# Scatter-add of scaled routed rows in a mixture-of-experts layer

## The chip, the cores and the metric

The kernel runs on one core of a Trainium2 chip. The metric is device time in microseconds (us) of one execution; before the change the median of three runs is 440.13 us (439.99 to 445.27).

## What is computed

A small vision tower: patches of 64 images are projected to 3136 tokens of 128 channels (B = 64 images, L = 49 tokens each), normalised, mixed along the tokens by a state-space convolution, and passed through a mixture of experts with 2 shared and 8 routed experts, of which each token takes the best two. The change is in this last part:

```python
hs = jax.nn.gelu(jnp.einsum('td,nfd->ntf', t, sw1) + sb1[:, None, :], approximate=False)
shared = jnp.einsum('ntf,ndf->td', hs, sw2) + sb2.sum(axis=0)
logits = t @ gate_w.T + gate_b
probs = jax.nn.softmax(logits, axis=-1)
top_v, top_i = jax.lax.top_k(probs, K)
cw = jnp.zeros_like(probs).at[jnp.arange(T)[:, None], top_i].add(top_v)
hr = jax.nn.gelu(jnp.einsum('td,efd->etf', t, rw1) + rb1[:, None, :], approximate=False)
oe = jnp.einsum('etf,edf->etd', hr, rw2) + rb2[:, None, :]
routed = jnp.einsum('etd,te->td', oe, cw)
return (shared + routed).reshape(b, s, d)
```

The layer's output is added to its input h. T is 3136, K is 2, F is 512.

## The kernel before

**Engines and order.** The program is written by hand: each engine has one list of instructions, and semaphores tie the lists together. Images come in and are projected in four tiles of 16 images (up to about 150 us), then comes the convolution, then the second normalisation (about 190 us) whose rows y are stored to the DRAM tensor yd, one row a token (store_y), and transposed for TensorE.

**Sorting the tokens.** VectorE picks each token's two experts (choose), counts ranks, and gives each of the 6272 (token, choice) pairs a slot in a list sorted by expert (sort_places). one_hots and TensorE's invert turn this into two tables with a column for each tile of 128 slots: take (which row of yd a slot reads) and give (which row of rd it writes); slot_tokens makes them. shares makes cwk, the two softmax shares of each token, for which ScalarE computes the Exp in step S_EXP of its list.

**Routed blocks.** The sorted list is cut into NB = 32 blocks of one expert each: 24 blocks of 256 slots (two tiles) and then 8 blocks of 128 slots (one tile); a table of 32 entries tells each block's expert. ORDER mixes these with the 16 pieces of shared work (8 groups of 392 tokens by 2 experts): 6 pieces first, then one after every three blocks. For a block i:

- SP loads the expert's weights into wb (load_weights, line 505, three buffers), once og of block i - 3 is complete.
- GpSimd gathers the rows of yd into xg, one indirect DMA a tile (gather, line 633, four buffers), and it issues the gather of block i + 4 ahead of the scatter of block i.
- TensorE transposes xg (line 1563), VectorE copies that to x32 (keep_x, line 1193), TensorE multiplies by the first weights (line 1505), ScalarE does the gelu (line 784), and TensorE multiplies by the second weights into PSUM bank 7 (line 1528). It may begin this when VectorE has read the last block's result from the bank.
- VectorE adds the expert's bias and writes og (rows_out, line 1200, two buffers); it waits for the scatter of block i - 2, which read the same buffer, to have landed.
- GpSimd scatters og's rows to rd, one indirect DMA a tile (scatter, line 640). rd has two rows for a token, one for each choice, and a row of its own for each empty slot. These scatters wait for nothing but og.

**The end.** When the last two blocks' scatters have landed, SP loads rk, both rows of each token, in 8 groups (load_routed, line 514, four buffers). ScalarE scales the first rows by their share (scale_routed, line 798), VectorE adds the scaled second rows to h (combine, line 1207) and then ScalarE's part (line 1212) into osb (two buffers), and SP stores osb (line 519) and loads a further group.

## Time and profile before

| | us |
|---|---|
| median of three runs | 440.13 |
| lowest, highest | 439.99, 445.27 |
| profiled execution | 444.05 |
| its span | 442.1 |
| busy: TensorE, ScalarE, VectorE, GpSimd | 364.2, 205.5, 183.0, 174.1 |

The profile is of one execution, which took 444.05 us; the hardware's records of it span 442.1 us. All instants below are counted from the span's start. Busy times leave out the issue of DMAs, except that GpSimd's indirect DMAs are counted while the engine makes them. In an instruction's row, the brackets give the time for which its engine had been idle before it, and what ended that. PE is TensorE, DVE is VectorE, ACT is ScalarE, POOL is GpSimd, and SPq is SP, which only issues DMAs.

### The profile page before, as it was taken

How to read it: one execution, taken by the hardware profiler on the slowest of the kernel's cores; microseconds unless marked ns; L12 is line 12 of the kernel's file. 1: busy time of each engine (PE TensorE's matmuls, PEld its weight loads, DVE VectorE, ACT ScalarE, POOL GpSimd, SP SyncE). 2: the span in 40 equal slices, each digit the busy share in tenths (PEclk: the TensorE clock that was granted, in tenths of full speed). 3: DMA queues.
4: the chain of work that ended last, by engine and by line, in shares of the span. 5: the costliest groups of instructions: out<-in, count | busy, mean ns of one | idle time of the engine just before them, and what ended most of it. 6: DMA issues, size and time to landing. Idle time of an engine off the chain costs nothing.

```text
span 442.1 us, 7120 instructions
## 1 busy us (share of the span) xinstructions
PE 364.2 (82%) x2490; PEld 299.8 (68%) x2490; DVE 183.0 (41%) x579; ACT 205.5 (46%) x424; POOL 174.1 (39%) x226
## 2 busy tenths in 40 slices
PE   0596998998967895839899999999999999989400
PEld 0465856666655784739777878988988988988300
DVE  0473485737769202392787221121121121121166
ACT  2660647837351631445563244554454445455153
POOL 7015134255221230062000357767767767654100
PEclk9995799998995697955798899999999999999855
DMA  8962046930010341022003015425435444455185
GB/s 209 265 191 74 16 131 165 312 128 0 1 71 40 122 150 60 1 74 73 0 33 130 19 42 210 159 101 212 156 128 183 161 146 166 172 173 187 29 278 149
DMA packets 22168, 54.38 MB, mean 123 GB/s; under 512 B 4551, under 2 KB 10109, under 8 KB 22137
## 3 DMA queue, kind: packets, MB, share of 16 engines
q1 hardware_dynamic: 17625, 46.25, 31.8%
q0 software_dynamic: 3968, 7.41, 6.0%
q10 hardware_dynamic: 544, 0.33, 0.4%
q8 instruction: 17, 0.28, 0.3%
q14 instruction: 14, 0.11, 0.1%
HBM read 28.10 MB, written 6.93 MB: 79 GB/s over the span
## 4 chain that ended last, share of the span: by engine, by line
PE 52%; issue 15%; DVE 12%; DMA 8%; POOL 4%; POOLq 3%; DVEq 3%; ACT 3%; SPq 1%; ACTq 0%
PE bank L1528 11%; PE bank L1505 11%; PE bank L1515 8%; DMA Xc<-in_x 3%; PE bank L1267 3%; PE bank L1300 3%; DVE dT L848 2%; PE bank L1480 2%; PE bank L1485 2%; PE bank L1486 2%; PE bank L1487 2%; DMA out<-osb 2%; DMA Tt<-kpad 1%; PE bank L1355 1%; PE bank L1563 1%
## 5 line engine op out<-in xcount | busy, mean ns | idle before, releaser
L633 POOL DMA_INDIRECT xg<-yd,take x56 | 54.5, 974 | 64.1 <-DVE give L1186 47.3
L784 ACT ACTIVATE gf<-bank,wb 128x256 f32<-128x256 f32 (+1 forms) x128 | 51.3, 447 | 52.6 <-PE bank L1505 52.6
L640 POOL DMA_INDIRECT rd<-og,give x56 | 55.2, 986 | 41.4 <-DVE og L1200 28.9
L1528 PE MATMUL bank<-wb,gf 128*128 128x128 f32 x448 | 55.4, 275 | 1.0 <-DVE og L1200 1.0
L1505 PE MATMUL bank<-x,wb 128*128 128x256 f32 (+1 forms) x256 | 54.0, 354 | 2.1 <-issue 1.2
L1528 PEld LDWEIGHTS bank<-wb,gf 128*128 128x128 f32 x448 | 53.2, 192 | 1.5 <-DVE og L1200 1.5
L784 ACT ACTIVATE gf<-bank,vcol 128x392 f32<-128x392 f32 x64 | 35.2, 588 | 36.5 <-PE bank L1487 36.5
L1505 PEld LDWEIGHTS bank<-x,wb 128*128 128x128 f32 x256 | 43.3, 191 | 9.3 <-issue 1.4
L1515 PE MATMUL bank<-gf,ws 128*128 128x392 f32 x128 | 44.8, 492 | 0.0
L1193 DVE COPY x<-bank 128x256 f32<-128x256 f32 (+1 forms) x32 | 12.5, 391 | 65.4 <-PE bank L1563 65.3
L1300 PE MATMUL bank<-patchT,Wp 128*128 128x392 f32 x96 | 38.4, 527 | 0.0
L1200 DVE TENSOR_TENSOR og<-bank,wb 128x256 f32<-128x256 f32 (+1 forms) x32 | 12.5, 390 | 54.6 <-PE bank L1528 50.4
L1515 PEld LDWEIGHTS bank<-gf,ws 128*128 128x128 f32 x128 | 23.3, 190 | 13.4
L1267 PE MATMUL bank<-ident,Xr 112*128 112x112 f32 x168 | 24.0, 288 | 5.6 <-ACT patchT L665 3.7
L1267 PEld LDWEIGHTS bank<-ident,Xr 112*128 112x128 f32 x168 | 19.7, 156 | 11.2 <-issue 6.1
L1485 PE MATMUL bank<-yh,ws 128*128 128x392 f32 x64 | 25.8, 404 | 0.0
L665 ACT COPY patchT<-bank 128x448 f32<-128x448 f32 (+1 forms) x48 | 21.2, 489 | 8.4 <-PE bank L1267 8.2
L1486 PE MATMUL bank<-yl,ws 128*128 128x392 f32 x64 | 24.0, 374 | 0.0
L1487 PE MATMUL bank<-yh,ws 128*128 128x392 f32 x64 | 23.7, 371 | 0.0
L676 ACT COPY Xr<-Xc 112x1792 f32<-112x1792 f32 x12 | 20.2, 1687 | 7.1 <-DMA Xc<-in_x 7.1
L1300 PEld LDWEIGHTS bank<-patchT,Wp 128*128 128x128 f32 x96 | 18.0, 208 | 8.1 <-issue 1.9
L1423 PE MATMUL bank<-Tt,u 98*32 98x98 f32 x256 | 19.9, 480 | 1.9 <-DMA Tt<-kpad 1.9
(266 smaller groups left out, 627.7 us busy)
## 6 DMA issues: line engine op xcount, KB each, us to landing
wb<-tab SPq DMA_DIRECT2D x32, 578.0 KB, 3.3
Xc<-in_x SPq DMA_DIRECT2D x12, 784.0 KB, 6.8
rk<-rd SPq DMA_DIRECT2D x8, 392.0 KB
Tt<-kpad SPq DMA_DIRECT2D x8, 300.1 KB
raw<-in_L_ffn_rw SPq DMA_DIRECT2D x1, 2048.0 KB, 10.2
out<-osb SPq DMA_DIRECT2D x8, 196.0 KB
Tt<-kpad SPq DMA_DIRECT2D x2, 600.2 KB
Tt<-kpad SPq DMA_DIRECT2D x1, 1200.5 KB
```

The lines of the kernel that those rows point to most:

```text
L633: G.indirect_dma_start(out=xg[i % AHEAD][:, t, :], out_offset=None, in_=yd[:, :], in_offset=bass.IndirectOffsetOnAxis(ap=take[:, at:at + 1 ...
L640: G.indirect_dma_start(out=rd[:, :], out_offset=bass.IndirectOffsetOnAxis(ap=give[:, at:at + 1], axis=0), in_=og[i % 2][:, t, :], in_offse ...
L665: nc.scalar.copy(patchT[:, t, lo:hi, :].rearrange("p w r -> p (w r)"), bank[i][:, 0:(hi - lo) * TR]).then_inc(tp_copied[i], 1)
L784: nc.scalar.activation(gf[q % 2][:, o, 0:width(q)], bank[o][:, 0:width(q)], ACT.Gelu, bias=bias1(n, o)).then_inc(act_done, 1)
L1267: return TP(dst, src, ident[0:rows_, 0:rows_])
L1300: last = MM(bank[2 + half][:, 0:GT], Wp[:, t, :], patchT[:, t, :, half * HR:(half + 1) * HR], start=t == 0, stop=t == KT - 1)
L1485: MM(dst_, hi_w, hi_x, start=start, stop=False)
L1486: MM(dst_, hi_w, lo_x, start=False, stop=False)
L1487: return MM(dst_, lo_w, hi_x, start=False, stop=stop)
L1505: last = MM(bank[o][:, 0:width(q)], wb[i % WB][:, FO + o * 128:FO + (o + 1) * 128], x32[i % 2][:, 0:width(q)], start=True, stop=True)
L1515: last = MM(bank[4][:, 0:GT], ws2[:, n % NS, o * D:(o + 1) * D], gf[q % 2][:, o, :], start=begin and o == 0, stop=last_ and o == FO - 1)
L1528: last = MM(bank[7][:, D * t:D * (t + 1)], gf[q % 2][:, o, 128 * t:128 * (t + 1)], wb[i % WB][:, FO + F + o * D:FO + F + (o + 1) * D], sta ...
```

## The change

The multiplication by the share moves from the end of the program into the blocks, and the addition of a token's two rows moves into the DMAs.

- yd gets rows of 130 elements: the last two are the token's two shares. SP stores them after the y rows from cwp, as 3136 pieces of two elements. shares now runs on VectorE between one_hots(0) and one_hots(1), and ScalarE's Exp one step sooner. GpSimd's gathers wait for that store too, and bring the shares along in xg.
- keep_x gets two small operations that choose the slot's share out of the two (kth marks which), into cws. A gather waits until they have read its buffer (cw_read).
- rows_out adds the bias as before, which frees TensorE's bank (down_read), and then multiplies each tile of og in SBUF by cws, before it signals og_ready.
- rd has one row a token, plus 256 rows for empty slots. SP clears it with zeros, between the image loads of the second and the third tile. The scatters add to it (compute_op is add). A token's two rows come from different blocks, so a block's scatters wait until those of the block before have landed.
- At the end SP issues all 8 loads of rk (8 buffers, half the bytes each) and then the stores (osb has four buffers). ScalarE does nothing there, and VectorE one addition a group.

```diff
-RKS = 4
+OSB = 4
+YW = D + 2
...
-S_EXP = 2
+S_EXP = 1
...
+        cwp = place("cwp", [PAIR, NPAIR, 2], "y")
+        kth = place("kth", [128, NQ, 2], "y")
+        cwt = place("cwt", [128, NQ, 2], "y")
+        cws = place("cws", [128, NQ], "y")
+        og = [place(f"og{i}", [128, TILES_OF, D], "y") for i in range(2)]
...
-        xg = [place(f"xg{i}", [128, TILES_OF, D], "x") for i in range(AHEAD)]
+        xg = [place(f"xg{i}", [128, TILES_OF, YW], "x") for i in range(AHEAD)]
...
-        rk = [place(f"rk{i}", [PAIR, GP, 2, D], "rk") for i in range(RKS)]
-        scl = [place(f"scl{i}", [PAIR, GP, D], "rk") for i in range(2)]
-        osb = [place(f"osb{i}", [PAIR, GP, D], "rk") for i in range(2)]
+        rk = [place(f"rk{i}", [PAIR, GP, D], "rk") for i in range(NG)]
+        osb = [place(f"osb{i}", [PAIR, GP, D], "rk") for i in range(OSB)]
...
-        yd = nc.dram_tensor("yd", [T, D], F32).ap()
-        rd = nc.dram_tensor("rd", [2 * T + SLOTS, D], F32).ap()
+        yd = nc.dram_tensor("yd", [T, YW], F32).ap()
+        rd = nc.dram_tensor("rd", [T + TILES_OF * 128, D], F32).ap()
...
+            for c in range(C):
+                sp_.wait_ge(x_sorted[c], 1)
+                load_x(1, c)
+            sp_.dma_start(rd[0:T, :].rearrange("(l a) d -> l a d", l=L),
+                          zeros[:, :].unsqueeze(1).broadcast_to([L, T // L, D])).then_inc(st_none, 16)
+            sp_.dma_start(rd[T:T + TILES_OF * 128, :].rearrange("(l a) d -> l a d", l=32),
+                          zeros[0:32, :].unsqueeze(1).broadcast_to([32, TILES_OF * 4, D])).then_inc(st_none, 16)
+            with sp_.Fori(2, TILES) as k:
                 for c in range(C):
                     sp_.wait_ge(x_sorted[c], k)
                     load_x(k, c)
 
             sp_.wait_ge(bias_ready, 1)
...
+            sp_.wait_ge(st_none, 32)
...
             def store_y(c):
                 sp_.wait_ge(y_ready[c % 2], c // 2 + 1)
-                dst_ = yd.rearrange("(i p) d -> i p d", p=NPAIR)[:, GP * c:GP * (c + 1), :]
+                dst_ = yd.rearrange("(i p) d -> i p d", p=NPAIR)[:, GP * c:GP * (c + 1), 0:D]
                 sp_.dma_start(dst_, ym[c][:, :, :]).then_inc(st_y, 16)
...
             def load_routed(c):
-                if c == 0:
-                    for i in range(2):
-                        sp_.wait_ge(scattered[i], moved(NB - 2 + i, 2))
-                if c >= RKS:
-                    sp_.wait_ge(out_ready, c - RKS + 1)
-                part = rd[0:2 * T, :].rearrange("(i p k) d -> i p k d", p=NPAIR, k=2)[:, GP * c:GP * (c + 1), :, :]
-                sp_.dma_start(rk[c % RKS][:, :, :, :], part).then_inc(ld_r[c % RKS], 16)
+                part = rd[0:T, :].rearrange("(i p) d -> i p d", p=NPAIR)[:, GP * c:GP * (c + 1), :]
+                sp_.dma_start(rk[c][:, :, :], part).then_inc(ld_r[c], 16)
 
             def store(c):
                 sp_.wait_ge(out_ready, c + 1)
                 dst_ = out.rearrange("b l d -> (b l) d")[GT * c:GT * (c + 1), :].rearrange("(p i) d -> i p d", p=GP)
-                sp_.dma_start(dst_, osb[c % 2][:, :, :]).then_inc(st_out[c % 2], 16)
+                sp_.dma_start(dst_, osb[c % OSB][:, :, :]).then_inc(st_out[c % OSB], 16)
 
             for c in range(NG):
                 store_y(c)
+            sp_.wait_ge(cw_ready, 1)
+            sp_.dma_start(yd.rearrange("(i p) d -> i p d", p=NPAIR)[:, :, D:YW], cwp[:, :, :]).then_inc(st_cw, 16)
             sp_.wait_ge(own_ready, 1)
             sp_.wait_ge(w_hi, 2 * NX)
             sp_.wait_ge(biases_in, 1)
             for i in range(NB):
                 load_weights(i)
-            for c in range(RKS):
+            for i in range(2):
+                sp_.wait_ge(scattered[i], moved(NB - 2 + i, 2))
+            for c in range(NG):
                 load_routed(c)
             for c in range(NG):
                 store(c)
-                if c + RKS < NG:
-                    load_routed(c + RKS)
-            for i in range(2):
-                sp_.wait_ge(st_out[i], 16 * NG // 2)
+            for i in range(OSB):
+                sp_.wait_ge(st_out[i], 16 * NG // OSB)
 
...
 
             def gather(i):
                 if i >= AHEAD:
-                    pool.wait_ge(tin_done, i - AHEAD + 1)
+                    pool.wait_ge(cw_read, i - AHEAD + 1)
                 for t in range(tiles_of(i)):
                     at = first_of(i) + t
                     G.indirect_dma_start(out=xg[i % AHEAD][:, t, :], out_offset=None, in_=yd[:, :],
                                          in_offset=bass.IndirectOffsetOnAxis(ap=take[:, at:at + 1], axis=0)).then_inc(gathered[i % AHEAD], 16)
 
             def scatter(i):
+
                 pool.wait_ge(og_ready, i + 1)
+                if i == 0:
+                    pool.wait_ge(give_ready, 1)
+                    pool.wait_ge(st_none, 32)
+                else:
+                    pool.wait_ge(scattered[(i - 1) % 2], moved(i - 1, 2))
                 for t in range(tiles_of(i)):
                     at = first_of(i) + t
                     G.indirect_dma_start(out=rd[:, :], out_offset=bass.IndirectOffsetOnAxis(ap=give[:, at:at + 1], axis=0),
-                                         in_=og[i % 2][:, t, :], in_offset=None).then_inc(scattered[i % 2], 16)
+                                         in_=og[i % 2][:, t, :], in_offset=None, compute_op=ALU.add).then_inc(scattered[i % 2], 16)
 
             pool.wait_ge(idx_ready, 1)
             pool.wait_ge(st_y, 16 * NG)
+            pool.wait_ge(st_cw, 16)
             for i in range(AHEAD):
                 gather(i)
...
-            def scale_routed(c):
-                act.wait_ge(ld_r[c % RKS], 16 * (c // RKS + 1))
-                if c >= 2:
-                    act.wait_ge(out_ready, c - 1)
-                for g in range(GP):
-                    p = GP * c + g
-                    last = nc.scalar.mul(scl[c % 2][:, g, :], rk[c % RKS][:, g, 0, :], cwk[:, 0, p:p + 1])
-                last.then_inc(scl_ready, 1)
-
...
                 dve.drain()
                 V.reciprocal(red[:, :], red[:, :])
                 dve.drain()
-                V.tensor_tensor(cwk[:, :, :], cwk[:, :, :], red[:, :].unsqueeze(1).broadcast_to([PAIR, 2, NPAIR]), ALU.mult)
+                V.tensor_tensor(cwp[:, :, :], cwk[:, :, :].rearrange("t k p -> t p k"), red[:, :].unsqueeze(2).broadcast_to([PAIR, NPAIR, 2]),
+                                ALU.mult).then_inc(cw_ready, 1)
 
...
-                V.tensor_scalar(inv[:, 1, :], inv[:, 1, :], 0.0, None, ALU.not_equal)
+                V.tensor_scalar(kth[:, :, :].rearrange("r q k -> r k q"), inv[:, :, :], 0.0, None, ALU.not_equal)
                 dve.drain()
...
-                dve.drain()
-                V.tensor_copy(take[:, :], srcf[:, :])
-                V.scalar_tensor_tensor(give[:, :], srcf[:, :], 2.0, inv[:, 0, :], ALU.mult, ALU.add).then_inc(idx_ready, 1)
+                dve.drain()
+                V.tensor_copy(take[:, :], srcf[:, :]).then_inc(idx_ready, 1)
+                V.tensor_tensor(give[:, :], srcf[:, :], inv[:, 0, :], ALU.add).then_inc(give_ready, 1)
 
             def keep_x(i):
...
                 V.tensor_copy(x32[i % 2][:, 0:n], bank[6][:, 0:n]).then_inc(x_ready, 1)
+                at = slice(first_of(i), first_of(i) + tiles_of(i))
+                V.tensor_tensor(cwt[:, at, :], xg[i % AHEAD][:, 0:tiles_of(i), D:YW], kth[:, at, :], ALU.mult).then_inc(cw_read, 1)
+                dve.drain()
+                V.tensor_reduce(cws[:, at], cwt[:, at, :], AX.X, ALU.add)
 
             def rows_out(i):
                 dve.wait_ge(down_done, AT[NSH + i] + 1)
@@ -1198,18 +1208,18 @@
                     dve.wait_ge(scattered[i % 2], moved(i - 2, 2))
                 n = tiles_of(i)
                 V.tensor_tensor(og[i % 2][:, 0:n, :], bank[7][:, 0:n * D].rearrange("p (t d) -> p t d", d=D),
-                                wb[i % WB][:, FO + F + FO * D:RW].unsqueeze(1).broadcast_to([128, n, D]), ALU.add).then_inc(og_ready, 1)
+                                wb[i % WB][:, FO + F + FO * D:RW].unsqueeze(1).broadcast_to([128, n, D]), ALU.add).then_inc(down_read, 1)
+                dve.drain()
+                for t in range(n):
+                    at = first_of(i) + t
+                    last = V.tensor_scalar(og[i % 2][:, t, :], og[i % 2][:, t, :], cws[:, at:at + 1], None, ALU.mult)
+                last.then_inc(og_ready, 1)
 
             def combine(c):
-                dve.wait_ge(ld_r[c % RKS], 16 * (c // RKS + 1))
-                for g in range(GP):
-                    p = GP * c + g
-                    V.scalar_tensor_tensor(h[:, p, :], rk[c % RKS][:, g, 1, :], cwk[:, 1, p:p + 1], h[:, p, :], ALU.mult, ALU.add)
-                dve.drain()
-                dve.wait_ge(scl_ready, c + 1)
-                if c >= 2:
-                    dve.wait_ge(st_out[c % 2], 16 * (c // 2))
-                V.tensor_tensor(osb[c % 2][:, :, :], h[:, GP * c:GP * (c + 1), :], scl[c % 2][:, :, :], ALU.add).then_inc(out_ready, 1)
+                dve.wait_ge(ld_r[c], 16)
+                if c >= OSB:
+                    dve.wait_ge(st_out[c % OSB], 16 * (c // OSB))
+                V.tensor_tensor(osb[c % OSB][:, :, :], h[:, GP * c:GP * (c + 1), :], rk[c][:, :, :], ALU.add).then_inc(out_ready, 1)
 
             for c in range(4):
...
                     one_hots(0)
+                    shares()
                     one_hots(1)
                 if q == S_TURN - 1:
                     one_hots(2)
                     one_hots(3)
                 if q == S_TURN:
                     slot_tokens()
-                if q == S_TURN + 1:
-                    shares()
             for c in range(NG):
...
                 if i >= 1:
-                    pe.wait_ge(og_ready, i)
+                    pe.wait_ge(down_read, i)
                 else:
                     pe.wait_ge(rank_read, 1)
```

GpSimd in the middle of the blocks, before. Each row is one indirect DMA, the name in brackets is the semaphore it waits for.

```order
L633 DMA xg_145<-yd,take 128x128
L640 DMA rd<-og_151,give 13440x128 [waits og_ready]
L640 DMA rd<-og_151,give 13440x128
L633 DMA xg_146<-yd,take 128x128 [waits tin_done]
L633 DMA xg_146<-yd,take 128x128
L640 DMA rd<-og_152,give 13440x128 [waits og_ready]
L640 DMA rd<-og_152,give 13440x128
```

The same place after:

```order
L644 DMA xg_151<-yd,take 128x130
L657 DMA rd<-og_116,give 3392x128 [waits scattered1,og_ready]
L657 DMA rd<-og_116,give 3392x128
L644 DMA xg_152<-yd,take 128x130 [waits cw_read]
L644 DMA xg_152<-yd,take 128x130
L657 DMA rd<-og_117,give 3392x128 [waits scattered0,og_ready]
L657 DMA rd<-og_117,give 3392x128
```

The order of gathers and scatters is the same. Each first scatter of a block now waits for the landing of the block before, with two gathers between them.

VectorE in the sort, before: the one_hots (Bm, Am, Av) of the first and second quarter, which TensorE's inversions read.

```order
L1165 TENSOR_TENSOR Bm0_175<-rowof_98,rh_133 98x2048
L1166 TENSOR_TENSOR Am0_177<-rowof_98,qh_132 98x896
L1169 TENSOR_TENSOR Av0_179<-Am0_177,idh_134 98x896
L1165 TENSOR_TENSOR Bm1_176<-rowof_98,rh_133 98x2048
L1166 TENSOR_TENSOR Am1_178<-rowof_98,qh_132 98x896
L1169 TENSOR_TENSOR Av1_180<-Am1_178,idh_134 98x896
```

The same place after:

```order
L1172 TENSOR_TENSOR Bm0_179<-rowof_98,rh_139 98x2048
L1173 TENSOR_TENSOR Am0_181<-rowof_98,qh_138 98x896
L1176 TENSOR_TENSOR Av0_183<-Am0_181,idh_140 98x896
L1102 TENSOR_REDUCE red_110<-pr_105 98x32
L1104 RECIPROCAL red_110<-red_110 98x32
L1106 TENSOR_TENSOR cwp_112<-cwk_111,red_110 98x64
L1172 TENSOR_TENSOR Bm1_180<-rowof_98,rh_139 98x2048
L1173 TENSOR_TENSOR Am1_182<-rowof_98,qh_138 98x896
L1176 TENSOR_TENSOR Av1_184<-Am1_182,idh_140 98x896
```

The three operations of shares, which stood behind give at the end of the sort, now stand ahead of the second quarter's one_hots.

## Rows read from the trace of the kernel before

**Rows 1.** The page, the chain that ended last, by engine.
```profile
PE 52%; issue 15%; DVE 12%; DMA 8%; POOL 4%; POOLq 3%; DVEq 3%; ACT 3%; SPq 1%; ACTq 0%
```
**Rows 2.** Busy time by stretch: us, PE, PEld, DVE, ACT, POOL, PEclk, DMA share, GB/s.
```profile
264.90:297.30 32.40, 32.40 (x202) 28.64 (x201) 6.17 (x14) 15.85 (x35) 23.58 (x24) 1.00 0.44 159
...
384.00:416.00 32.00, 29.13 (x194) 24.97 (x192) 6.47 (x19) 14.87 (x43) 13.63 (x15) 1.00 0.43 143
418.20:442.10 23.90, 0.00 (x0) 0.00 (x0) 14.03 (x40) 10.14 (x32) 0.00 (x0) 0.50 0.67 202
```
**Rows 3.** Who waited for whom, 240 to 420 us: total, times, longest.
```profile
POOL rd L640 <- DVE og L1200: 28.9, 15, 5.5
...
DVE og L1200 <- DMA rd<-og,give: 4.2, 1, 4.2
```
**Rows 4.** GpSimd in order of time: start, duration, engine, instruction, idle before.
```profile
265.03 1.01 POOL L640 DMA_INDIRECT rd<-og,give  x1 [3.65 <-DVE og L1200]
...
297.40 0.99 POOL L640 DMA_INDIRECT rd<-og,give  x1 [1.78 <-DVE og L1200]
...
334.87 1.00 POOL L640 DMA_INDIRECT rd<-og,give  x1 [0.30 <-issue]
336.17 0.99 POOL L640 DMA_INDIRECT rd<-og,give  x1 [0.30 <-issue]
...
340.02 1.00 POOL L640 DMA_INDIRECT rd<-og,give  x1 [0.30 <-issue]
```
**Rows 5.** The gathers of line 633, from issue to landing.
```profile
DMA to landing us min/median/max: 2.5/2.8/5.6
```
**Rows 6.** The end, all engines in order of time.
```profile
414.40 0.97 POOL L640 DMA_INDIRECT rd<-og,give  x1 [5.47 <-DVE og L1200]
...
415.95 0.97 POOL L640 DMA_INDIRECT rd<-og,give  x1 [0.58 <-DVE og L1200]
418.24 1.62 SPq L514 DMA_DIRECT2D rk<-rd  x4
...
422.19 1.14 DVE L1207 SCALAR_TENSOR_TENSOR h<-rk,cwk,h 98x128 f32<-98x128 f32 x4 [6.52 <-DMA rk<-rd]
...
423.63 1.28 ACT L798 ACTIVATE scl<-rk,cwk 98x128 f32<-98x128 f32 x4 [0.17 <-DMA rk<-rd]
424.11 1.13 DVE L1207 SCALAR_TENSOR_TENSOR h<-rk,cwk,h 98x128 f32<-98x128 f32 x4
...
438.59 0.69 DVE L1212 TENSOR_TENSOR osb<-h,scl 98x512 f32<-98x512 f32 x1
```
**Rows 7.** The sort: ScalarE, TensorE, VectorE and GpSimd in order of time.
```profile
223.15 2.19 ACT L784 ACTIVATE gf<-bank,vcol 128x392 f32<-128x392 f32 x4 [4.40 <-PE bank L1487]
...
235.12 1.97 PE L1552 MATMUL bank<-Av,Bm 98*128 98x56 f16 x16 [0.40 <-DVE Av L1169]
...
248.61 0.42 DVE L1096 TENSOR_REDUCE red<-pr 98x32 f32<-98x256 f32 x1
...
249.53 0.23 DVE L1100 TENSOR_TENSOR cwk<-cwk,red 98x64 f32<-98x64 f32 x1
...
248.99 1.14 POOL L633 DMA_INDIRECT xg<-yd,take  x1 [47.32 <-DVE give L1186]
```
**Rows 8.** Line 897, duration of one in ns (min/median/max).
```profile
L897 DVE TENSOR_SCALAR xtok<-xtok,mv,rstd x32: 339/342/348, 55.0 to 136.1; 98x128 f32<-98x128 f32 x32
```
**Rows 9.** SP: the store of 196 pieces, and the load that waits for it.
```profile
145.29 0.27 SPq L484 DMA_DIRECT2D kpad<-ksb  x1
146.81 2.02 SPq L478 DMA_DIRECT2D Tt<-kpad  x4
```
**Rows 10.** VectorE in a block: idle before the copy and before og.
```profile
298.04 0.43 DVE L1193 COPY x<-bank 128x256 f32<-128x256 f32 x1 [0.92 <-PE bank L1563]
299.83 0.42 DVE L1200 TENSOR_TENSOR og<-bank,wb 128x256 f32<-128x256 f32 x1 [1.36 <-PE bank L1528]
```
**Rows 11.** Busy time by stretch, while the third tile's images come.
```profile
40.00:50.00 10.00, 10.00 (x111) 8.57 (x111) 2.57 (x11) 2.49 (x6) 0.00 (x0) 0.56 0.00 1
```

More of the change, by code:

```diff
@@ L239, in tower @@
         assert end["y"] <= end["b"], (end["y"], end["b"])
-        xg = [place(f"xg{i}", [128, TILES_OF, D], "x") for i in range(AHEAD)]
+        xg = [place(f"xg{i}", [128, TILES_OF, YW], "x") for i in range(AHEAD)]
         x32 = [place(f"x32{i}", [D, BLK], "x") for i in range(2)]
-        og = [place(f"og{i}", [128, TILES_OF, D], "x") for i in range(2)]
         ymx = [place(f"ymx{i}", [PAIR, GP, D], "x") for i in range(4)]
@@ L327, in tower @@
         scattered = [sem(f"scattered{i}") for i in range(2)]
-        ld_r = [sem(f"ld_r{i}") for i in range(RKS)]
-        st_zero, st_k, st_out = sem("st_zero"), sem("st_k"), [sem(f"st_out{i}") for i in range(2)]
-        st_y = sem("st_y")
+        ld_r = [sem(f"ld_r{i}") for i in range(NG)]
+        st_zero, st_k, st_out = sem("st_zero"), sem("st_k"), [sem(f"st_out{i}") for i in range(OSB)]
+        st_y, st_cw, st_none = sem("st_y"), sem("st_cw"), sem("st_none")
+        cw_ready, cw_read, give_ready, down_read = sem("cw_ready"), sem("cw_read"), sem("give_ready"), sem("down_read")
         lsrep_ready, par_T, ls_T, vec_T = sem("lsrep_ready"), sem("par_T"), sem("ls_T"), sem("vec_T")
@@ L363, in tower @@
         tin_done, x_ready, og_ready = (sem(n) for n in ("tin_done", "x_ready", "og_ready"))
-        scl_ready, out_ready = sem("scl_ready"), sem("out_ready")
+        out_ready = sem("out_ready")
         block = ctx.enter_context(nc.Block())
@@ L452, in _ @@
             sp_.dma_start(skip[L - 1:L, :], D_.unsqueeze(0)).then_inc(ld_skip, 16)
-            with sp_.Fori(1, TILES) as k:
+            for c in range(C):
[6 more added lines that the diff above has]
+            with sp_.Fori(2, TILES) as k:
                 for c in range(C):
@@ L608, in _ @@
             G.iota(idf[:, :], [[1, NPAIR]], base=-(T // 2), channel_multiplier=NPAIR, allow_small_or_imprecise_dtypes=True)
-            G.iota(dump[:, :], [[128, NQ]], base=T, channel_multiplier=1, allow_small_or_imprecise_dtypes=True)
+            G.iota(dump[:, :].rearrange("r (q t) -> r q t", t=TILES_OF), [[0, NQ // TILES_OF], [128, TILES_OF]], base=T - T // 2, channel_multiplier=1,
+                   allow_small_or_imprecise_dtypes=True)
             G.iota(rowof[:, :, :], [[1, 128], [0, JG]], base=0, channel_multiplier=0, allow_small_or_imprecise_dtypes=True)
@@ L826, in _ @@
                         high_y(c)
-            for c in range(NG):
-                scale_routed(c)
         @block.vector
@@ L1562, in transpose_in @@
                 for t in range(tiles_of(i)):
-                    last = TP(bank[6][:, 128 * t:128 * (t + 1)], xg[i % AHEAD][:, t, :], ident[:, :])
+                    last = TP(bank[6][:, 128 * t:128 * (t + 1)], xg[i % AHEAD][:, t, 0:D], ident[:, :])
                 last.then_inc(tin_done, 1)
```

1 line of the change is left out of this document (removed).

## The prediction

> **What bounds the kernel now.** I read the page's chain of waits first, then busy time by stretch, then the waits, and then the instructions in order of time at three places. The chain [rows 1] says that TensorE holds half of it and that DMA, VectorE and "issue" share the rest; it does not say where. The stretches do [rows 2]. In the routed phase, from about 265 to 384 us, TensorE is busy for the whole stretch and GpSimd for 23.58 of 32.40 us. From 384 to 416 us, where the blocks are one tile wide, TensorE still works 29.13 of 32.00 us. From 418.2 us to the end TensorE does nothing: this tail of 23.9 us is loads of the routed rows, VectorE, ScalarE and stores. So there are two limits: TensorE until 415 us, the tail after it.
>
> GpSimd's 73% is misleading. In order of time [rows 4] its four indirect DMAs of a block start 1.29 us apart: 0.99 busy and 0.30 to the next. A two-tile block costs it 4 x 1.29 = 5.15 us (334.87 to 340.02). The program needs one block in 5.40 us: 265.03 to 297.40 is 32.37 us for six blocks. GpSimd's slack is 0.25 us a block, seen as one wait of 1.78 us in six. The waits [rows 3] say the same from the other side: GpSimd waited for og only 15 times in 56, and VectorE once, for 4.2 us, for a scatter to land. GpSimd is a hidden second limit, and the change adds its wait exactly there.
>
> **The tail, and what the change takes from it.** Before [rows 6]: the last scatter is issued at 415.95, the first load of rk at 418.24, its rows are used at 422.19, and the last addition runs from 438.59 to 439.28; its store ends the span at 442.1. Per group VectorE does four STTs and one addition, 1.14 + 0.69 us, with small gaps 1.9 us (422.19 to 424.11), and stores delay two of them; 8 groups need 17 us.
>
> After: ScalarE's eight scalings and 32 STTs are gone, and one addition of 0.69 us (0.75 with its gap) stays for each group. Half the bytes are read. Before, the second load was usable 1.44 us after the first (422.19, 423.63) for 392 KB, or 272 KB/us. I take 196 KB in 0.72 us. The first load took 3.95 us from issue, of which 1.44 was its data, so its half is usable after 3.2 us. All eight loads are issued ahead, so the last is there at 3.2 + 7 x 0.72 = 8.2 us after the final landing. Additions 0 to 3 keep pace with the loads, but their stores stand behind all eight loads in SP's queue, and addition 4 needs store 0 to have landed (four osb buffers): 8.2, plus 0.72 for its data, plus about 1.3 us for completion (415.95 + 0.97 to 418.24), or 10.2. Four more additions end at 13.0, and the last store needs 2.8 (439.28 to 442.1). That is 15.8; since completion and data overlap in part I take 15.6 against 23.9: **8.3 us saved**. The floor is 3.2 MB at 272 KB/us plus completion, 11.8 + 2.0 = 13.8, or 10.1 saved.
>
> **The scatters' wait.** Let A be the time from the start of a block's second scatter to the landing of both. The next block's scatter can't start before A is over. Before, the two gathers between them already kept it 3.85 us away (336.17 to 340.02), and there is the slack of 0.25. So A up to 4.1 us costs nothing in the two-tile blocks. Behind a waiting scatter on GpSimd stand the next gathers, which have four blocks of lead, and the scatters behind them; VectorE's write of og, two blocks later, waits for the landing, then TensorE's next down-projection waits for VectorE. The order pieces in the section on the change show that only the wait is new; no instruction of GpSimd moves.
>
> An accumulating scatter doesn't occur in this trace. A plain one takes 2.29 us by that measure (415.95 to 418.24); a read of rows from HBM takes 2.8 us from issue to landing [rows 5]. The floor is 2.29, since the old row has to be read first. The ceiling is both one after the other, 5.1. Less the gather's own issue of 0.99 the read is worth at most 1.8, and part of this is the way back of a completion, which the scatter has too. I take 1.0 for the read: **A = 3.3 us**, nearer to the plain scatter, and inside the 4.1.
>
> It still costs at the end, where nothing covers it. Before, the last two scatters start at 414.40 and 415.95 and land at 418.24 [rows 6]. After: og is complete about 0.35 later (the new multiplication, below), the first starts at 414.75 and lands at 418.05, the second starts at 418.1 and lands at 421.4. **+3.2 us.** With A = 2.29 it would be +1.2.
>
> If A is long: every block costs 1.30 + A + 0.05. At A = 4.6 this is 5.95, or 0.55 over 5.40, x 24 blocks = 13.2, less about 3 us which the two og buffers absorb once. The one-tile blocks have 30.7/8 = 3.84 us each (384.7 to 415.4, from the stretch in [rows 2]) and would need 4.65: + 6.5. The last landing adds 2.3. Together +19. At the ceiling 5.1: 25 - 3 + 10.5 + 2.8 = +35.
>
> **VectorE's new work.** Per two-tile block: two multiplications of 128x128. The nearest row is a TENSOR_SCALAR of 98x128 from SBUF, 0.34 us [rows 8]; with the drain some 0.75 us. Before x is copied VectorE has waited 0.92 us at the tightest place [rows 10], so the copy isn't late. The two small operations behind the copy (128x4 and 128x2, some 0.4 us) fit into the 1.36 us before the next og [rows 10]. TensorE is released by the first, unscaled write (down_read), as before. Cost 0, but og_ready is late by 0.75 (0.35 for one tile); this counts only at the end, above.
>
> **The shares, moved forward.** They take 248.61 to 249.76 us now [rows 7], beside TensorE's work. The diff puts them between the first and the second one_hots (the order pieces of VectorE at the sort). TensorE waits there for VectorE: it began the second inversion at 235.12 after waiting 0.40 us for Av. So these 1.15 us, less the gap that they share with their neighbours, go on the path: **+1.1 us**. ScalarE's Exp moves one step forward, into the 4.40 us for which ScalarE waited for TensorE before 223.15: 0.
>
> **The 8-byte pieces.** The shares are stored as 3136 pieces of 8 bytes behind the y rows, and SP's first three loads of weights and GpSimd's first gather (248.99, [rows 7]) come after them. The nearest row is a store of 196 pieces of 128 bytes that landed within 1.52 us [rows 9]. Purely by pieces this would be 24 us; if 1.3 of it is the fixed completion of the last scatter, 3.5 us more. I take 8 us: issued at about 234, landed by 242. Hidden by the inversion until 249. The ceiling would put the first gather at 258, +9.
>
> The Trainium skill (DMA: Bandwidth & Descriptors, Specifications) says that pieces under 512 bytes make the DMA engine read, modify and write. No row here has pieces of 8 bytes to HBM; by that rule this term leans to its ceiling, and I leave it a chance of its own.
>
> **Clearing rd** writes 1.6 MB of zeros behind the second tile's image loads. From 40 to 50 us the DMA engines stand idle [rows 11] and the next tile's images are sorted after that: 0, at most 3. Gathered rows grow by 8 bytes: 0.
>
> **Sum.** -8.3 + 3.2 + 1.1 = -4.0 us. The profiled execution took 444.05 us (span 442.1 and 1.95 around it), so 440.05; it was slower than the median of 440.13. Taken from the median: **436.1 us**.
>
> **Rivals.**
> 1. The landings take the place of GpSimd's slack (A of 4.3 and more). For it: an addition in memory is a read and a write, each paying its way, and the weights' loads share the engines (DMA share 0.44, [rows 2]); the longest landing of a gather was 5.6, [rows 5]. Against it: a gather's 2.8 is measured under that same load. Place: each scatter's start, from A = 4.1 on. At A = 4.6: 440.13 - 8.3 + 19 + 1.1 = 452. It ends slower.
> 2. GpSimd's issues get longer. The new multiplications read and write SBUF alone, which in the routed phase none of VectorE's large operations did (they read PSUM). If GpSimd is held up while they run, each block costs it 0.68 us more: 5.83 against 5.40, 0.43 x 24 = 10.3 less 3, so 436.1 + 7.3 = 443.4. Descriptors for an addition may also take longer to make than 0.99 us, with the same effect. The Trainium skill (SBUF — State Buffer, Who interferes with whom) states this: a tensor_scalar in a two-port mode blocks GpSimd, and with it the writing of descriptors. No row here shows the two side by side.
> 3. The 8-byte pieces take over 15 us and hold up the first gathers and weights: up to +9, 445.
> 4. All small terms fall well: the tail at its floor (-10.1), the landing at 2.29 (+1.2), half of the shares hidden (+0.5): 431.7, or a little less.
>
> **How the numbers follow.** The forecast has 0.45, rival 1 0.33, rival 2 0.10, rival 3 0.05, rival 4 0.07. Two per cent, about what a measurement of this kernel can tell from no change, is 431.3 to 448.9 us. Of rival 1 the part below A = 4.5 (448.6) stays within it, and at high A rival 2 adds to it: slower 0.32. Faster by over 2% needs more than rival 4's sum: 0.08. The rest, 0.60, is within. The range reaches from rival 4's floor to rival 1 with A = 4.85 (+27 instead of +19): 430.5 to 460. The forecast's own range, with A from 2.3 to 4.0, is 432 to 441.
>
> **What would show it.** The tail from the last landing of rd should be 14.5 to 16.5 us, with the fifth addition waiting for a store. The time from the second scatter to the next block's first should stay near 3.85, GpSimd's six blocks at 32.4 us, and VectorE's og should seldom wait for rd. The last two scatters should lie 3.3 us apart. TensorE's wait before its second inversion should be 1.5 instead of 0.4 us. I am wrong if six blocks take over 33 us: with indirect DMAs of 0.99 us and waits for rd it is rival 1, with longer ones rival 2; and wrong in another way if the first gather starts after 251 us.

## The result: slower, 473.3 us against 440.7

The changed kernel takes 473.33 us (median of 4 runs, 470.59 to 477.02), the kernel before beside it 440.71 (4 runs, 439.99 to 445.27). The ratio is 1.0724, 95% interval 1.0622 to 1.0826. On a second chip it was 471.47 (2 runs) against 440.37, ratio 1.0711 (1.0627 to 1.0794). The forecast was 436.1 and the range ended at 460: wrong in size and sign.

The page of the changed kernel, the chain that ended last, by engine and then by line; its counterpart is [rows 1]:

```profile
DMA 24%; issue 20%; PE 17%; POOL 17%; DVE 12%; DVEq 3%; POOLq 3%; ACT 2%; SPq 1%; ACTq 0%
DMA rd<-og,give 18%; POOL rd L657 10%; POOL xg L644 3%; PE bank L1276 3%; PE bank L1309 2%; DMA gbb<-in_L_ffn_gate_b 2%; DVE dT L854 2%; PE bank L1489 2%; PE bank L1514 2%; PE bank L1364 1%; PE bank L1524 1%; DMA Tt<-kpad 1%; DMA out<-osb 1%; PE bank L1561 1%; POOL QT L599 1%
```

TensorE held half of the chain and now holds 17%. The scatters have its place, as transfers (18%) and as instructions of GpSimd (10%).

GpSimd of the changed kernel in order of time, one two-tile block and the start of the next (line 657 is the scatter, 644 the gather); compare [rows 4]:

```profile
301.43 1.63 POOL L657 DMA_INDIRECT rd<-og,give  x1 [0.64 <-issue]
303.37 1.59 POOL L657 DMA_INDIRECT rd<-og,give  x1 [0.30 <-issue]
305.26 1.02 POOL L644 DMA_INDIRECT xg<-yd,take  x1 [0.30 <-issue]
306.58 0.98 POOL L644 DMA_INDIRECT xg<-yd,take  x1 [0.30 <-issue]
307.87 1.63 POOL L657 DMA_INDIRECT rd<-og,give  x1 [0.30 <-DVE og L1215]
```

The idle time before a scatter is mostly the 0.30 us of before. What grew is the scatter itself, from 0.99 to 1.6 us, while a gather stays at 0.98 to 1.02. A block is 6.44 us of GpSimd (301.43 to 307.87) where it was 5.15 and 5.40 are needed.

Line 657 as one group, the changed kernel: durations in ns, who waited for its transfers, and its landings:

```profile
L657 POOL DMA_INDIRECT rd<-og,give x56: 1552/1587/1663, 268.4 to 455.5; - x56
...
DVE og L1210: 80.7, 23
POOL rd L657: 25.9, 14
...
DMA to landing us min/median/max: 3.2/3.9/5.0
```

All 56 are long, even the shortest (1552 ns). VectorE's write of og waited 80.7 us for landings; it was 4.2 before [rows 3]. VectorE and behind it TensorE wait for a queue that GpSimd can't empty in time. (The last row counts from a scatter's start to its landing.)

Busy time by stretch, the changed kernel: six blocks, the one-tile blocks, the tail; columns as in [rows 2]:

```profile
268.36:307.87 39.51, 37.41 (x234) 32.62 (x233) 12.23 (x44) 18.47 (x39) 31.29 (x25) 1.00 0.57 145
```
```profile
423.80:455.60 31.80, 19.55 (x124) 15.64 (x123) 6.13 (x26) 8.50 (x25) 14.06 (x11) 0.91 0.41 96
458.86:474.20 15.34, 0.00 (x0) 0.00 (x0) 5.38 (x8) 0.00 (x0) 0.00 (x0) 0.50 0.70 209
```

Six blocks take 39.51 us instead of 32.37. In the one-tile blocks TensorE is busy 61% instead of 91%. The tail is 15.34 instead of 23.9.

The one-tile blocks of the changed kernel, VectorE and GpSimd in order of time:

```profile
423.25 0.29 DVE L1210 TENSOR_TENSOR og<-bank,wb 128x128 f32<-128x128 f32 x1 [4.26 <-DMA rd<-og,give]
...
423.88 1.58 POOL L657 DMA_INDIRECT rd<-og,give  x1 [2.06 <-DMA rd<-og,give]
...
427.94 0.29 DVE L1210 TENSOR_TENSOR og<-bank,wb 128x128 f32<-128x128 f32 x1 [4.02 <-DMA rd<-og,give]
...
428.58 1.58 POOL L657 DMA_INDIRECT rd<-og,give  x1 [1.79 <-DMA rd<-og,give]
```

Here the new wait does bind: 4.70 us from scatter to scatter where TensorE needs 3.84. The landing of the scatter at 423.88 lets VectorE go at 427.94, after 4.06 us, and GpSimd's next scatter 0.64 us later. Wherever both wait for one landing, GpSimd goes on 0.63 to 0.67 us behind VectorE. Towards the end the landing is seen by VectorE after 3.38 us (447.43 to 450.81), and the scatters are 4.0 to 4.1 us apart.

The end of the changed kernel; its counterpart is [rows 6]:

```profile
451.45 1.55 POOL L657 DMA_INDIRECT rd<-og,give  x1 [2.47 <-DMA rd<-og,give]
455.55 1.55 POOL L657 DMA_INDIRECT rd<-og,give  x1 [2.54 <-DMA rd<-og,give]
458.86 3.38 SPq L522 DMA_DIRECT2D rk<-rd  x8
461.68 1.52 DVE L1222 TENSOR_TENSOR osb<-h,rk 98x512 f32<-98x512 f32 x2 [10.19 <-DMA rk<-rd]
...
468.22 2.62 DVE L1222 TENSOR_TENSOR osb<-h,rk 98x512 f32<-98x512 f32 x4 [2.33 <-DMA out<-osb]
```

**Where the 32.1 us are** (span 474.2 against 442.1). First scatter at 268.36 instead of 265.03: +3.3. From there to the first scatter of the last two-tile block (417.05, before 385.19), 148.7 instead of 120.2: +28.5. From that scatter to the last landing (458.86), 41.8 instead of 33.05: +8.8. Tail: -8.5.

The first +3.3 is not all the change's. In a repeat of the kernel before, the same store of y rows began 2.25 us later than in the run shown (195.83 instead of 193.58), so single executions differ by that much before the change touches anything. Counted from that store to the first scatter, before takes 71.5 and 71.1 us, and the five executions with the shares moved forward on chips where the kernel before took 440 us take 73.1 to 73.8: **+2.2 us**.

### The profile page after: what moved, and what is told of

Its sections match the earlier page's. It is cut to its first block, busy times and chain, and to the rows that moved or that the text cites. A ratio compares the mean times of both kernels' runs of the same rounds, so it can differ in the third digit from the quotient of the medians.

```text
span 474.2 us, 7250 instructions
## 1 busy us (share of the span) xinstructions
PE 374.2 (79%) x2490; PEld 300.7 (63%) x2490; DVE 196.1 (41%) x666; ACT 197.0 (42%) x392; POOL 210.4 (44%) x226
## 3 DMA queue, kind: packets, MB, share of 16 engines
q0 software_dynamic: 10240, 7.47, 12.6%
## 4 chain that ended last, share of the span: by engine, by line
DMA 24%; issue 20%; PE 17%; POOL 17%; DVE 12%; DVEq 3%; POOLq 3%; ACT 2%; SPq 1%; ACTq 0%
DMA rd<-og,give 18%; POOL rd L657 10%; POOL xg L644 3%; PE bank L1276 3%; PE bank L1309 2%; DMA gbb<-in_L_ffn_gate_b 2%; DVE dT L854 2%; PE bank L1489 2%; PE bank L1514 2%; PE bank L1364 1%; PE bank L1524 1%; DMA Tt<-kpad 1%; DMA out<-osb 1%; PE bank L1561 1%; POOL QT L599 1%
## 5 line engine op out<-in xcount | busy, mean ns | idle before, releaser
L657 POOL DMA_INDIRECT rd<-og,give x56 | 89.6, 1599 | 42.4 <-DMA rd<-og,give 25.9
L644 POOL DMA_INDIRECT xg<-yd,take x56 | 56.0, 999 | 65.9 <-DVE take L1191 49.1
L1514 PE MATMUL bank<-x,wb 128*128 128x256 f32 (+1 forms) x256 | 55.5, 360 | 9.3 <-DVE x L1199 8.0
L1537 PE MATMUL bank<-wb,gf 128*128 128x128 f32 x448 | 57.4, 281 | 3.7 <-DVE og L1210 3.5
L1210 DVE TENSOR_TENSOR og<-bank,wb 128x256 f32<-128x256 f32 (+1 forms) x32 | 12.5, 391 | 92.0 <-DMA rd<-og,give 80.7
L1276 PEld LDWEIGHTS bank<-ident,Xr 112*128 112x128 f32 x168 | 20.2, 159 | 11.7 <-issue 6.7
L575 POOL TENSOR_TENSOR rstd<-mv,eps 98x8 f32<-98x8 f32 x8 | 1.7, 206 | 50.1 <-DVE mv L862 50.1
L694 ACT COPY Xr<-Xc 112x1792 f32<-112x1792 f32 x12 | 20.2, 1687 | 6.8 <-DMA Xc<-in_x 6.8
```

The costliest lines, as they stand in the source:

```text
L644: G.indirect_dma_start(out=xg[i % AHEAD][:, t, :], out_offset=None, in_=yd[:, :], in_offset=bass.IndirectOffsetOnAxis(ap=take[:, at:at + 1 ...
L657: G.indirect_dma_start(out=rd[:, :], out_offset=bass.IndirectOffsetOnAxis(ap=give[:, at:at + 1], axis=0), in_=og[i % 2][:, t, :], in_offse ...
L1276: return TP(dst, src, ident[0:rows_, 0:rows_])
L1514: last = MM(bank[o][:, 0:width(q)], wb[i % WB][:, FO + o * 128:FO + (o + 1) * 128], x32[i % 2][:, 0:width(q)], start=True, stop=True)
L1537: last = MM(bank[7][:, D * t:D * (t + 1)], gf[q % 2][:, o, 128 * t:128 * (t + 1)], wb[i % WB][:, FO + F + o * D:FO + F + (o + 1) * D], sta ...
```

## The experiments

Theory I: the adding scatter takes GpSimd longer to issue, by itself. Theory L: VectorE's new multiplications in SBUF hold GpSimd up (the first half of the forecast's rival 2). Rival 1 of the forecast puts the loss on the landings.

**Plain scatters, wait kept.**

```diff
-                in_=og[i % 2][:, t, :], in_offset=None, compute_op=ALU.add)
+                in_=og[i % 2][:, t, :], in_offset=None)
```

> The changed kernel with plain scatters in place of adding ones, the wait between blocks kept (a token's two rows then overwrite each other, so the addition is left out). Theory I (the adding DMA takes GpSimd longer to issue: 1.6 us in place of 0.98): scatters are back at 0.98 us, a two-tile block at 5.4 us, and the time is 440.7 + 3.3 (before the first scatter) - 8.5 (tail) + 1.5 (last two landings) = 437 us. Theory L (VectorE's multiplications in SBUF hold GpSimd up while it writes descriptors): scatters stay at 1.6 us and the time above 465 us. Theory W (the wait itself costs, whatever lands): 23 waits on VectorE for a scatter stay, above 450 us.

Scatters took 967/986/1004 ns (min/median/max), as before, with all multiplications in place: theory L falls and I holds for the issue. The time, 477.74 us, decided nothing: on this chip the kernel before itself took 476.29 (462.75 to 480.98), and on the fourth experiment's chip 466.40 (one run). In the traces of two kernels with plain scatters from this chip, VectorE and ScalarE wait for long stretches that the profile puts down to nothing on the core ("remote", 29.0 us for og in this run). Why is not known, and no trace of the kernel before was taken there. So from these two chips only durations of instructions are used, and times of kernels that GpSimd bounds.

**No multiplication.**

```diff
-                for t in range(n):
-                    ...
-                    last = V.tensor_scalar(og[i % 2][:, t, :], og[i % 2][:, t, :], cws[:, at:at + 1], None, ALU.mult)
-                last.then_inc(og_ready, 1)
+                dve.wait_ge(down_read, i + 1)
+                V.memset(none[:, 0:1], 0.0).then_inc(og_ready, 1)
```

> The changed kernel without VectorE's multiplication of og by the share (left out of the result); adding scatters and the wait stay. Theory I: scatters stay at 1.6 us and the time at 472 us, within 1.5 us. Theory L: scatters at 0.98 us and below 445 us.

1552/1586/1647 ns: VectorE's multiplications cost GpSimd's issues nothing. The time is 474.08 us (472.93 and 475.23), near the 473.33 with them and half a microsecond outside what I expected. Counted from the first store of y rows to the end, it is 277.0 us against 279.1 and 278.3 in two traces of the changed kernel, so they may cost the kernel up to some 2 us; this is too near the spread to tell.

**Adding scatters, no wait, two rows a token.** Each scatter adds to a cleared row of its own, so none has to wait for another.

```diff
-                else:
-                    pool.wait_ge(scattered[(i - 1) % 2], moved(i - 1, 2))
...
+                V.scalar_tensor_tensor(give[:, :], srcf[:, :], 2.0, inv[:, 1, :], ALU.mult, ALU.add).then_inc(give_ready, 1)
```

> The changed kernel with two rows a token in rd, so that no two scatters add to the same row and the wait between blocks goes; the adding stays. rd is cleared whole (6.9 MB in place of 1.7), and at the end only the first row of a token is read and added (the second is left out). Theory I: two-tile blocks stay at 6.43 us (2 x 1.93 + 2 x 1.30), only the one-tile blocks and the last scatters get shorter, by 6 to 9 us: 465 us, plus what the longer clearing costs ahead of the blocks. Theory W (the landing is what costs): two-tile blocks back to 5.4 us and 440 us.

466.21 us (465.42 to 467.08), scatters 1552/1587/1657 ns. GpSimd in order of time:

```profile
299.25 1.63 POOL L659 DMA_INDIRECT rd<-og,give  x1 [0.30 <-issue]
301.19 1.59 POOL L659 DMA_INDIRECT rd<-og,give  x1 [0.30 <-issue]
303.08 1.02 POOL L648 DMA_INDIRECT xg<-yd,take  x1 [0.30 <-issue]
304.40 0.98 POOL L648 DMA_INDIRECT xg<-yd,take  x1 [0.30 <-issue]
305.69 1.63 POOL L659 DMA_INDIRECT rd<-og,give  x1 [0.30 <-issue]
```

Without the wait a block is still 6.44 us, and VectorE's write of og still waits 60.8 us for landings. The issue is as long as in the changed kernel although no two scatters touch the same row, so it isn't the adding to shared rows either.

| us | before | adding, no wait | changed |
|---|---|---|---|
| first scatter to that of the last two-tile block | 120.2 | 143.0 | 148.7 |
| from there to the last scatter | 30.8 | 30.2 | 38.5 |
| both | 150.9 | 173.2 | 187.2 |

(Adding, no wait: 273.51, 416.53 and 446.73.) In the two-tile blocks the issue costs 22.9 us and the wait 5.7. Only 1.0 of the 5.7 falls in the first 17 of the 23 intervals. The other 4.7 fall in the last six, where the blocks to be gathered have one tile and only one gather stands between two blocks' scatters. In the one-tile blocks the longer issue by itself costs nothing and the wait 8.3. So of the 36.3 us between first and last scatter 22.3 are the issue's and 14.0 come with the wait for adding landings, where I had expected 6 to 9. The whole time fell by less, to 466.21 us, because the longer clearing (41 us of issue on SP) pushed everything back: the first store of y rows came at 199.48 instead of 195.09.

**Four forms of the scatter, one after the other by block.**

```diff
-                    G.indirect_dma_start(... give[:, at:at + 1] ... in_=og[i % 2][:, t, :] ... compute_op=ALU.add)
+                    # i % 4: 0 add, 128 rows; 1 add, 64 rows; 2 plain, 128 rows; 3 plain, 64 rows
```

> The changed kernel with its scatters in four forms by block number modulo 4: adding 128 rows, adding 64 rows, plain 128 rows, plain 64 rows (so part of the rows and of the additions is left out); the wait between blocks stays. It measures the issue on GpSimd and the landing of each form by itself. If the longer issue belongs to each adding row, 64 adding rows take about half of the 0.61 us more (plain 64: some 0.75 us, adding 64: 1.05 us); if it is a fixed step, adding 64 rows take 0.6 us more than plain 64. Landing from the start of the second scatter: plain 2.3 us, adding 3.3 to 4.3 us.

Line by line, 14 of each, mean ns second:

```profile
L658 POOL DMA_INDIRECT rd<-og,give x14 | 22.6, 1616 | 21.9 <-DVE og L1225 17.1 <-issue 2.4 <-DMA rd<-og,give 2.3
...
L661 POOL DMA_INDIRECT rd<-og,give x14 | 20.4, 1455 | 14.3 <-DMA rd<-og,give 8.5 <-DVE og L1225 3.2 <-issue 2.6
...
L664 POOL DMA_INDIRECT rd<-og,give x14 | 13.7, 982 | 11.7 <-DVE og L1225 5.0 <-issue 4.9 <-DMA rd<-og,give 1.8
...
L667 POOL DMA_INDIRECT rd<-og,give x14 | 12.8, 914 | 10.0 <-issue 7.2 <-DMA rd<-og,give 2.8
```

Adding costs 0.63 us more for 128 rows and 0.54 for 64. Halving the rows takes little off either: most of it is a step per instruction. (Estimate by a straight line through the two: 0.45 us a step, and 1.4 ns a row.) This is one execution, and its time (472.12 us) isn't used. Landings could be read in the last blocks: adding 64 rows 3.05 us (445.33 to VectorE's og at 448.38), plain 64 rows 2.22 (452.08 to the loads at 454.30).

**Plain scatters of scaled rows to two rows a token, no wait.** The whole layer is computed; the tail reads both rows, with loads of 392 KB and two additions a group.

```diff
-                    pool.wait_ge(scattered[(i - 1) % 2], moved(i - 1, 2))
...
-                                         in_=og[i % 2][:, t, :], in_offset=None, compute_op=ALU.add)
+                                         in_=og[i % 2][:, t, :], in_offset=None)
...
+                V.tensor_tensor(part, part, rk[c % 4][:, :, 0, :], ALU.add)
```

> The share is multiplied in the blocks as in the change, but the scatters are plain, without the wait, to two rows a token as before; rd isn't cleared; at the end VectorE adds both rows (two additions of 0.69 us a group in place of four 0.28 us operations and one), ScalarE does nothing. All is computed. Theory I: the blocks run at 5.4 us as before, the tail is bound by 4.8 MB at 272 KB/us plus 2 us, 19.7 us in place of 23.9, and the sort costs 1.1 to 2 us: 438 us. A rival: the tail is bound by VectorE and the stores as before and nothing is won, 441 to 443 us.

The first try (478.97 us against 476.29 for the kernel before) fell on the same chip as the first experiment. It was repeated on another, with both kernels:

> The kernel before, unchanged, for its trace on the chip of this comparison. In the comparisons so far it took 462 to 481 us where its first runs took 440, and kernels with GpSimd in front (adding scatters) didn't move. If TensorE is what is slower there, the trace shows ScalarE and VectorE waiting for matmuls that end late, in stretches where GpSimd is idle, and unchanged issues on GpSimd (0.98 us); if DMAs are, loads of wb take longer than 3.3 us. On a chip like the first it takes 440 us and shows neither.

> The changed kernel, unchanged, beside the kernel before on the same chip. GpSimd sets its blocks (6.43 us each), which has slack against TensorE (5.40), so it should take 471 to 477 us on any chip; against the kernel before 7% slower where that takes 440, and within 3% of it where that takes 465 to 475.

> The version with two rows a token and plain scatters again, beside both kernels: 2 to 4 us faster than the kernel before on the same chip (tail 19.7 us in place of 23.9, sort 1.1 to 2 us dearer), if the chip is steady enough to show it; in the trace the tail from the last landing of rd to the end is 18.5 to 20.5 us.

Here the kernel before takes 440 us and shows none of the late waits, so that question stays open. Against itself it has the ratio 0.9989. After: 471.47, as above. The two-row version: 440.38 us (10 runs), ratio 0.9988 (0.9954 to 1.0022): the 33 us are gone, but the 2 to 4 us that I expected are not won. Its tail is 20.2 us (422.30 to 442.5), 3.7 shorter than before, but it reaches its first scatter 2.3 to 2.7 us later, counted from the y rows' store.

**Plain scatters, wait kept, on another chip.**

> The same kernel as in the first experiment: after the change, but with plain scatters in place of adding ones, the wait for the last block's scatters kept. It leaves the addition of a token's two rows out (the last writer stays). The chip of the first experiment could not time it. Terms now, against the kernel before (440.4 us): the tail 15.4 instead of 23.9 us (-8.5), the shares and their store ahead of the first gather +1.6 (yd's store to first gather is 57.0 us after the change, 55.3 before), the last two scatters kept apart by a plain landing +1.2. Theory I (the issues of 1.6 us on GpSimd cost what the sum lacked; the wait as such costs nothing where a landing takes 2.3 us): indirect DMAs of 0.98 us, six two-tile blocks in 32.4 us, tail 15.4, time 434.7 us (432 to 438). Theory W (the wait chains GpSimd's queue and costs time with plain landings too): six blocks over 33 us or one-tile blocks over 4.2 us each, GpSimd waiting for rd in many blocks, time 442 us or more.

437.61 us (12 runs) against 440.59, ratio 0.9926 (0.9891 to 0.9961). Six blocks of this kernel, columns as in [rows 2], and its last scatters and loads in order of time:

```profile
264.35:296.75 32.40, 32.40 (x203) 28.68 (x202) 10.77 (x38) 15.84 (x35) 23.60 (x25) 1.00 0.46 160
```
```profile
413.37 0.97 POOL L657 DMA_INDIRECT rd<-og,give  x1 [2.48 <-DVE og L1215]
...
416.34 0.97 POOL L657 DMA_INDIRECT rd<-og,give  x1 [2.00 <-DMA rd<-og,give]
418.64 3.37 SPq L522 DMA_DIRECT2D rk<-rd  x8
```

Theory I is right and theory W falls: TensorE is busy in all of the 32.40 us, and from the first scatter to the last it takes 152.0 us against 150.9 before. With plain landings the wait costs 1.1. They aren't all 2.3 us: VectorE saw one after 3.80 (402.11 to 405.91). The last two scatters are 2.97 us apart (413.37 to 416.34) with a landing of 2.30 (416.34 to 418.64), so here too some 0.7 us pass between a landing and GpSimd's next scatter. The whole change without the word "add" would have gained 3.0 us (1.7 to 4.8), the forecast's sign and nearly its size; but then a token's second row overwrites its first. The terms (tail -8.5, wait +1.1, way to the first scatter +2.2) add up to -5.2, somewhat more than was gained; where the rest went wasn't found.

**The two-row version in float16.** Scaled rows are written, stored and read back as float16; all eight loads fit and go out at once.

```diff
-                V.tensor_tensor(part, part, rk[c % 4][:, :, 0, :], ALU.add)
+                V.tensor_tensor(rk[c][:, :, 0, :], rk[c][:, :, 0, :], rk[c][:, :, 1, :], ALU.add)
```

> A version that may beat both: plain scatters of scaled rows to two rows a token as in the two-row version, no wait, but the scaled rows are written, stored and read back as float16, so all eight loads of both rows fit beside each other and go out at once; VectorE adds the two halves in float16 and then the sum to h. Rows of 256 bytes. Theory I: nothing but the tail changes against the two-row version (span 442.5, tail 20.2): scatter issues stay 0.97 us, the tail becomes 15.0 us (3.2 to the first load, then 8 groups of 1.1 us or 0.72 us a load, the fifth addition behind a store, 2.8 for the last store), so 440.4 - 5.2 = 435.2 us (433 to 438). Theory S (scattered rows of 256 bytes cost the DMA engines more than rows of 512): scatters land later than 2.3 us or the tail's loads come later than with 512-byte rows, 438 to 442 us.

437.46 us (12 runs), ratio 0.9925 (0.9893 to 0.9957): it beats both kernels, the one before by 3 us. It gives up precision of the routed rows for this. Its end in order of time:

```profile
415.69 0.97 POOL L646 DMA_INDIRECT rd<-oh,give  x1 [0.57 <-DVE oh L1206]
417.90 3.38 SPq L515 DMA_DIRECT2D rk<-rd  x8
420.46 0.42 DVE L1211 TENSOR_TENSOR rk<-rk 98x512 f16<-98x512 f16 x1 [5.05 <-DMA rk<-rd]
...
428.54 0.69 DVE L1215 TENSOR_TENSOR osb<-h,rk 98x512 f32<-98x512 f32 x1 [2.33 <-DMA out<-osb]
...
431.83 0.69 DVE L1215 TENSOR_TENSOR osb<-h,rk 98x512 f32<-98x512 f32 x1
```

The last landing is seen after 2.21 us, so here 256-byte rows cost nothing against 512 (2.29); the tail is 17.7 us (417.90 to 435.6) instead of the 15.0 I expected. The loads pace the first additions, as expected, but the additions after the fifth's wait take 1.1 us each, where the changed kernel's take 0.65.

## Why the prediction was wrong

**Where the limit is: right.** GpSimd's 5.15 of 5.40 us a block was the number that mattered, and "the change adds its wait exactly there" pointed at the right queue.

**The failed step: "a block costs it 4 x 1.29".** The forecast carried the plain scatter's 0.99 us over to the adding one, which takes 1.59. It named the operation as absent from the trace, and bounded its landing from both sides, but its issue only in half a sentence of rival 2, at a tenth of the chance and with the size of another mechanism (+0.68 us a block). It is +1.29, 6.44 for 5.15, and so 1.04 over the 5.40 that a block had. By the run without the wait this is 22.9 us of the loss (1.04 x 23 would be 24). The order of instructions hid it: no instruction moved, two of four became another instruction.

**Rival 2: its first mechanism wrong, its second right.** The second, descriptors that take longer to make, was given the same price as the first, +0.68 us a block, and had nearly twice that. For the first, the Trainium skill (SBUF — State Buffer, Who interferes with whom) says that a tensor_scalar in a two-port mode blocks GpSimd. No run here shows whether this multiplication runs in such a mode. The runs show nothing of a delay: 986 ns with multiplications and plain scatters, against 984 before, and 1586 without multiplications against 1587 with them. In the changed kernel the gather at 306.58 above is 0.98 us long with two multiplications (307.29, 0.48 us) beside its end. Nor was it new that VectorE works from SBUF beside GpSimd. The kernel before has a large operation on two tiles in SBUF, five times between 240 and 420 us, which the prediction overlooked:

```profile
294.21 0.56 DVE L1040 TENSOR_TENSOR yl<-yf,yh 128x392 fp32r<-128x392 f32 x1
```

**The wait: half right.** The landing A is 3.31 us at the very end (455.55 to 458.86), the 3.3 of the forecast. Most landings of a block's second scatter are near it: in the two-tile blocks those that VectorE waited for were seen after 3.3 to 4.2 us (once 4.85), half of them within 3.4. The first one-tile blocks have 4.1 to 4.3. The forecast had one value for all of them. It also let GpSimd's next scatter start 0.05 us after a landing; it starts 0.64 us behind VectorE, so at least that much after it. So "the last two scatters should lie 3.3 us apart" was 4.10 although A was right, and a one-tile block takes 4.06 + 0.64 = 4.70 where 3.35 would have fitted into the 3.84. Why GpSimd goes on later than VectorE wasn't tried. In a two-tile block with two gathers in between, the longer issue itself covers most of the wait: 4.50 us from the second scatter to the next (303.37 to 307.87), against 3.4 and 0.64 in the middle and 4.2 and 0.64 at the long end. With plain issues the gap would be 3.85, so the two costs can't simply be taken apart and added for other kernels. The wait comes to 14.0 us of the 36.3, shown by the run without it, and the last landing is 1.0 us longer on top (3.31 for 2.29); the forecast had 3.2 for all of this. Rival 1 was thus real, in its smaller place.

**The tail: right**, -8.5 for -8.3, with the fifth addition waiting for a store (2.33 us).

**The shares: right, with a rest.** TensorE, the changed kernel, second inversion ([rows 7] had 0.40):

```profile
237.67 1.96 PE L1561 MATMUL bank<-Av,Bm 98*128 98x56 f16 x16 [1.46 <-DVE Av L1176]
```

That is +1.06 for +1.1. But the way to the first scatter grew by 2.2. Counted from the store of y rows, +1.0 is there at the second inversion (four executions), +1.5 at the first gather and +2.2 at the first scatter (means of the same five executions against the two of before). What the other 1.1 us are wasn't tried; the store of the shares, the wider y rows and VectorE's sort all lie in that way.

**The 8-byte pieces: hidden, as forecast.** The first gather waited for VectorE's take until 252.47, with the shares' store issued at 235.27, so it had landed within 17 us; the forecast's 8 us is neither shown nor refuted. The row of SP:

```profile
235.27 0.97 SPq L532 DMA_DIRECT2D yd<-cwp  x1
```

**VectorE's multiplications: right** for GpSimd's issues, and at most some 2 us for the kernel (the run without them). **Clearing rd** was taken out by itself in no run. The first store of y rows came at 190.2 to 196.1 us in six executions with the clearing of the change and at 191.0 to 195.8 in five without it, so no cost shows in that spread.

With the terms read from the two traces the sum is 440.7 + 2.2 + 28.5 + 8.8 - 8.5 = 471.7 us, against 471.5 and 473.3 measured. That it closes says only that no stretch was left out; which part is whose comes from the experiments.

## What to carry to other kernels

When a change swaps one form of an instruction for another on an engine with a few per cent of slack, price its issue as well as its transfer, and give an unmeasured issue a range of its own. A wait costs by the landing it waits for, and by the time the waiting engine takes to go on: here 1.1 us in all with plain landings, 14 with adding ones. Saving a read at the end is worth little where it makes every write dearer: two plain rows a token and a cheaper addition at the end do as well, and with smaller rows better.

## What the hardware showed that I had not expected

- An adding indirect DMA of 128 rows of 512 bytes occupies GpSimd 1.59 us, a plain one 0.98; most of the difference stays with 64 rows (1.45 against 0.91).
- It is also sent differently. The software queue's packets, the changed kernel and then the one with plain scatters:

```profile
q0 software_dynamic: 10240, 7.47, 12.6%
```
```profile
q0 software_dynamic: 3968, 7.47, 6.5%
```

The bytes are the same. 10240 - 3968 = 6272 = 56 x 16 x 7, which fits each of 16 engines sending eight packets, one a row, instead of one; this is inferred from the counts.
- Its landing takes 3.2 to 5.0 us from its start, 3.3 at the quiet end; a plain one's is 2.3 there, and VectorE saw one of 3.8 before.
- A scatter that waits for a landing starts 0.64 us after VectorE's operation that waits for the same one, for the changed kernel as for the one with plain scatters (0.65, 405.91 to 406.56).
